# Two batches through attention and MLP layers: side work of one batch placed between the attention slots of the other

## The chip, the cores and the metric

One NeuronCore of a Trainium2 chip. The metric is the device time of one execution in microseconds (us). Several executions of a kernel are timed and their median is given; one further execution is profiled, and all rows in this document come from profiled executions.

## The reference, cut to what matters

B = 2 batches, S = 512 tokens, D = 128 features. `x` passes through four conditioned layers; the change touches only what follows layer 0.

```python
def L1(x, c):                       # attention over all tokens, then a 4-chunk MLP
    h = ln(x) * (1 + scale_msa) + shift_msa
    q, k, v = split(h @ w_qkv)      # 16 heads of 8 features
    x = x + gate_msa * (softmax(q @ k.T * 8 ** -0.5) @ v @ w_proj + b_proj)
    h2 = ln(x) * (1 + scale_mlp) + shift_mlp
    return x + gate_mlp * (gelu(h2 @ w_fc1 + b_fc1) @ w_fc2 + b_fc2)

def L2(x, t, mask):                 # two 2-chunk MLPs, the first one masked
    norm = where(m, ln(x) * (1 + scale) + shift, 0)
    x = x + gate * where(m, gelu(norm @ ssm_w1 ..) @ ssm_w2 + gelu(norm @ bwd_w1 ..) @ bwd_w2, 0)
    return x + gate_mlp * (gelu_tanh(ln'(x) @ ff_w1 + ff_b1) @ ff_w2 + ff_b2)

def L3(x, c):                       # as L1, but the attention is causal
    ...
```

## The kernel before, in words

Every engine runs its own instruction stream; they wait for one another on semaphores. Layer 0 (quantised products, a scan, a gated MLP) takes the first 170 us and is the same before and after.

Then comes a sequence of six blocks, `SEQ` (line 213): number 0, attention of layer 1, called here the open attention (a = 0); numbers 1, 2 and 3, MLPs of 4, 2 and 2 chunks of 128 hidden features; number 4, the causal attention of layer 3 (a = 1); number 5, a 4-chunk MLP. Each block is done for both batches before the next one begins. Chunks are columns of the hidden layer: a first-layer product (L1376) makes one chunk for all 512 tokens, an activation (L1186) applies Gelu or its tanh form and writes `hid`, and the second-layer products (L1529) make the result, four token tiles by as many chunks. Each batch's MLP is preceded by a norm: statistics on VectorE (L516, L519, L521), the inverse root on GpSimd (L344), the normalised `xn` on VectorE (L526), four transposes on TensorE (L1247), and the modulated `hT` on ScalarE (L1125).

An attention has eight units, four heads of one batch each; units 0 to 3 are batch 0, units 4 to 7 batch 1. A unit has eight slots, each with two score products in bf16 (L1497, keys by queries) and two exponentials on ScalarE (L1173). Every second slot completes a key tile, whose product with the values, P·V (L1475, fp32), is accumulated in one bank over four key tiles. In the causal attention key tile kt concerns only queries from 128 kt on, so its score products, exponentials and P·V are 512, 384, 256 and 128 wide, and GpSimd zeroes the triangle first (L440).

The exponentials need each row's maximum beforehand. It is taken from a second set of score products, queries by keys (L1451; in the causal attention with a mask product, L1454), by a VectorE reduction (L932): eight steps per unit, six in the causal attention. GpSimd splits the maxima into bf16 parts (L430 to L432), TensorE transposes them (`parts`, L1421), VectorE copies them, and SyncE writes them by DMA into rows of `QZ` (L329), so that the score product subtracts the maximum itself. q and k stand in `QZ` and `KZ` as three bf16 pieces each: ScalarE makes the high part (L1136) and the middle (L1140), VectorE the rests (L808, L812), and SyncE copies the pieces into place with twelve DMAs per batch (L321), issued one after the other.

PSUM has eight banks. Three (2, 3, 4) hold scores for the exponentials, one (5) the accumulated output, and two pairs (0 and 1, 6 and 7) are a ring (`RING`, line 237). Every other result in an attention is a ring item and takes the next pair in turn; a new item waits for what was read out of the item two before it (`consumed`, line 1395).

The order of the ring items is written out by `schedule` (line 240): the maxima run 12 steps ahead of the slots (9 in the causal attention), the split maxima are transposed one maximum after a unit is complete (`LAG`, line 228), the output of a unit is transposed and divided in slot 5 of the unit after next, and a few items of batch 0 come early (`EARLY`, line 230): its output transposed in slot 52, its projection in 54, its next norm transposed in 59. P·V is issued in two halves of the queries (`probs_out`, line 1458), one per slot, from three or four slots behind (`LATE`, line 229). ScalarE copies the output of unit u-1 before the exponentials of slot 3 of unit u (`unit_out`, line 1141). Before ScalarE changes its function a small activation loads the function table ahead of need (`table`, line 1043).

GpSimd also adds the gated bias to `x` (`add_bias`, line 393). For MLP 2 it does so tile by tile, a product with the mask (L398) and an add (L399), sixteen instructions, each waited for.

```python
SEQ = ((0, "att", 1), (1, "mlp", 1), (2, "mlp", 2), (3, "mlp", 3), (4, "att", 3), (5, "mlp", 5))
advance(min(ahead + ((s + 1) * n + 7) // 8 - (0 if s >= 39 else 0), first + (s + 1) * n // 5))
for s in range(64):
    # two score products, then the ring items of the slot, then half a P.V
```

## Time and profile before

| what | value |
|---|---|
| median of 3 timed executions | 490.38 us (489.73 to 490.95) |
| profiled execution, own time | 488.39 us |
| profiled execution, span of its instructions | 486.6 us |
| mean granted TensorE clock | 0.825 of full |
| layer 0 and the first q, k, v | 0 to about 175 us |
| exponentials of the open attention | 195.4 to 285 us |
| MLPs 1 to 3, second q, k, v, first causal maxima | 285 to 360 us |
| exponentials of the causal attention | 360.4 to 461.3 us |
| output, projection, last MLP, store | 461.3 to 486.6 us |

Times in rows are microseconds from the first instruction of the span. Own time less span, 1.8 us, lies outside the instructions. A group row counts one line of the kernel on one engine; `L1475 x8` are eight instructions, since an fp32 product is two. The granted clock is TensorE's: 1.00 is 2.4 GHz and 0.50 is 1.2 GHz. In a chain, each piece is what the next one waited for.

### The profile page before, as it was taken

The numbers are of one execution on the slowest core, as the hardware profiler recorded it, in microseconds if no ns is written. First come the engines' busy times: TensorE is split into PE (matmuls) and PEld (weight loads), VectorE is DVE, ScalarE is ACT, GpSimd is POOL, SyncE is SP. The second block draws the span as 40 slices with busy tenths as digits, with TensorE's granted clock in tenths as the row PEclk, the third lists the DMA queues.
The fourth block names the chain that finished last, engine by engine and source line by source line (L and its number), as shares of the span: only waits on it lengthen the run. The fifth ranks groups of instructions, "written<-read, shape, count | busy, mean of one in ns | idle before, by whom it ended". The sixth has DMA issues, their size and how long they took to land.

```text
span 486.6 us, 6451 instructions
## 1 busy us (share of the span) xinstructions
PE 317.5 (65%) x2274; PEld 148.4 (31%) x2274; DVE 303.9 (62%) x683; ACT 251.0 (52%) x550; POOL 121.9 (25%) x184
## 2 busy tenths in 40 slices
PE   0015844621245563988988888758678977788786
PEld 0004613511103420222222345535222232333354
DVE  0778787759588659888888314346675354554230
ACT  3267645562466212788887773333435354456542
POOL 0112139640363510000000202563012222222410
PEclk9999965555557756799999999989757598889799
DMA  7940350000000233000000000000710000000001
GB/s 243 417 186 0 130 223 0 1 0 0 1 0 1 68 99 92 2 3 3 1 2 2 2 2 1 0 1 20 198 43 2 1 2 3 2 1 2 1 1 43
DMA packets 11652, 21.90 MB, mean 45 GB/s; under 512 B 2010, under 2 KB 10462, under 8 KB 10846
## 3 DMA queue, kind: packets, MB, share of 16 engines
q1 hardware_dynamic: 11620, 21.49, 12.8%
q8 instruction: 18, 0.29, 0.2%
q14 instruction: 14, 0.11, 0.1%
HBM read 14.54 MB, written 0.52 MB: 31 GB/s over the span
## 4 chain that ended last, share of the span: by engine, by line
PE 41%; DVE 24%; ACT 18%; POOL 6%; issue 6%; DMA 2%; SPq 2%; DVEq 0%; ACTq 0%; POOLq 0%
PE pe L1475 10%; ACT big L1173 8%; PE pe L1497 6%; DVE nm L932 5%; PE pe L1376 4%; PE pe L1529 4%; PE pe L1451 4%; PE pe L1454 3%; PE pe L1247 2%; POOL rstd L344 2%; ACT scr L1058 2%; PE pe L1341 2%; PE pe L1426 1%; DVE st L516 1%; DVE xn L526 1%
## 5 line engine op out<-in xcount | busy, mean ns | idle before, releaser
L1173 ACT ACTIVATE big<-pe 128x512 f32<-128x512 f32 (+3 forms) x256 | 116.7, 521 | 81.6 <-PE pe L1497 80.4
L932 DVE TENSOR_REDUCE nm<-pe 128x2 f32<-128x1024 f32 (+2 forms) x112 | 124.2, 1145 | 50.1 <-PE pe L1454 38.1
L1475 PE MATMUL pe<-big,scr 128*32 128x256 f32 (+4 forms) x896 | 74.1, 408 | 3.8 <-ACT scr L1146 2.6
L1451 PE MATMUL pe<-big 62*128 62x512 bf16 (+3 forms) x256 | 53.1, 395 | 15.9 <-DVE nm L932 13.0
L1497 PE MATMUL pe<-big 64*128 64x512 bf16 (+3 forms) x256 | 54.9, 371 | 8.4 <-ACT big L1173 7.0
L344 POOL TENSOR_TENSOR rstd<-var,half 128x4 f32<-128x4 f32 x26 | 28.5, 1097 | 110.5 <-DVE var L521 85.9
L440 POOL TENSOR_SCALAR_AFFINE_SELECT big<-big 128x512 f32<-128x512 f32 x32 | 20.3, 635 | 73.4 <-ACT big L1173 73.4
L1497 PEld LDWEIGHTS pe<-big 64*128 64x128 bf16 x256 | 15.7, 94 | 64.7 <-ACT big L1173 33.5
L430 POOL CAST nm<-nm 128x16 bf16<-128x16 f32 x16 | 3.1, 196 | 102.0 <-DVE nm L932 102.0
L526 DVE TENSOR_SCALAR xn<-x_tok,mv,rstd 128x128 f32<-128x128 f32 x64 | 18.6, 353 | 15.7 <-POOL rstd L344 15.7
L1475 PEld LDWEIGHTS pe<-big,scr 128*32 128x32 f32 x896 | 18.9, 111 | 29.2 <-issue 12.3
L1125 ACT ACTIVATE hT<-pe,modc 128x512 f32<-128x512 f32 x12 | 9.4, 779 | 34.7 <-PE pe L1247 34.7
L1247 PE MATMUL pe<-ident,xn 128*128 128x128 f32 x48 | 9.4, 330 | 26.7 <-ACT xn L1058 13.6
L1376 PE MATMUL pe<-hT,w 128*128 128x512 f32 x48 | 24.5, 636 | 3.5 <-ACT hT L1125 3.5
L1247 PE MATMUL pe<-ident,scr 128*128 128x128 f32 x48 | 12.8, 431 | 19.2 <-ACT scr L1058 18.2
L1186 ACT ACTIVATE scr<-pe,col 128x512 f32<-128x512 f32 x24 | 16.3, 688 | 14.6 <-PE pe L1376 14.6
L1451 PEld LDWEIGHTS pe<-big 62*128 62x128 bf16 x256 | 13.4, 98 | 30.0 <-DVE nm L932 20.6
L1454 PE MATMUL pe<-cmask 128*128 128x128 bf16 x128 | 21.5, 260 | 0.0
L955 DVE RECIPROCAL rec<-pe 128x16 f32<-128x16 f32 x16 | 4.0, 252 | 22.6 <-PE pe L1426 22.6
L1050 ACT ACTIVATE junk<-scr 128x128 f32<-128x128 f32 x24 | 7.1, 297 | 20.6 <-DVE scr L649 20.5
L1058 ACT ACTIVATE scr<-scr,magic,q 128x128 f32<-128x128 f32 x32 | 12.7, 480 | 9.5 <-DVE q L670 9.5
L969 DVE TENSOR_TENSOR x_tok<-x_tok,pe 128x512 f32<-128x512 f32 x6 | 4.1, 688 | 21.1 <-PE pe L1529 21.0
(188 smaller groups left out, 560.3 us busy)
## 6 DMA issues: line engine op xcount, KB each, us to landing
big<-tern SPq DMA_DIRECT2D x48, 128.0 KB, 2.4
big<-in_fill SPq DMA_DIRECT2D x1, 4096.0 KB, 13.6
big<-in_wa SPq DMA_DIRECT2D x1, 2304.0 KB, 12.5
w<-in_w SPq DMA_DIRECT2D x2, 1152.0 KB, 19.2
big<-in_wa SPq DMA_DIRECT2D x1, 1344.0 KB, 6.2
big<-in_w SPq DMA_DIRECT2D x1, 1024.0 KB, 14.4
w<-in_w SPq DMA_DIRECT2D x1, 896.0 KB, 19.8
rowg<-in_rowg SPq DMA_DIRECT2D x1, 832.0 KB, 18.4
```

Of the source, the lines that this page charges most:

```text
L344: nc.gpsimd.tensor_tensor(dst, src, half[0:src.shape[0], 0:n], ALU.pow).then_inc(sem(done), 1)
L440: nc.gpsimd.affine_select(block_, block_, [[0, HG], [1, 128]], ALU.is_ge, zero, base=0, channel_multiplier=-1).then_inc(sem("triangle"), 1)
L526: last = v.tensor_scalar(xn[:, t], x_tok[:, t], mv[:, t, 0:1], rstd[:, t:t + 1], ALU.subtract, ALU.mult)
L932: v.tensor_reduce(dst, src[:, :, 0:w * len(pairs)].rearrange("p r (h w) -> p r h w", w=w), AX.X, ALU.max, negate=True).then_inc(sem(f"a{a} ...
L1058: last = s_.activation(dst[:, t], src[:, t], ACT.Identity, bias=magic[:, 0:1], scale=q4[:, 3, m, t:t + 1])
L1173: s_.activation(P[:, kt % PRING, 2 * p + j, q0:S], bank[SINGLES[i % 3]][:, q0:S], ACT.Exp, scale=SCALE).then_inc(sem(f"a{a}_p"), 1)
L1247: last = t_.transpose(bank[bk][:, i * D:(i + 1) * D], src[:, t], ident[:])
L1376: t_.matmul(bank[2 + i % 4], m["w"][:, m["at"] + c * D:m["at"] + (c + 1) * D], hT[:, b], start=True, stop=True).then_inc(sem("n_h"), 1)
L1451: last = t_.matmul(dsts[par][:, k * wd:(k + 1) * wd], QZ[rows, b, 2 * g + i, qt * 128:(qt + 1) * 128], KZ[rows, b, 2 * g + i, 0:wd], start ...
L1454: last = t_.matmul(dsts[par][:, (k + 1) * wd - 128:(k + 1) * wd], cmask[:, 0], cmask[:, 1], start=False, stop=True)
L1475: last = t_.matmul(bank[PV_BANK][32 * h:32 * h + 32, lo:hi], V[b][:, kt, HG * g + h, :], P[:, k % PRING, h, lo:hi], start=(kt == 0), stop= ...
L1497: last = t_.matmul(bank[SINGLES[(2 * s + j) % 3]][:, q0:S], KZ[rows, b, 2 * g + p, kt * 128:(kt + 1) * 128], QZ[rows, b, 2 * g + p, q0:S], ...
```

## The change

The whole of `SEQ` is replaced by one list of events, `ORDER`, made by `work_order()`, that all five engines walk. Between the slots of an attention stand events of the MLPs (`SIDE`), for a batch whose attention is already done:

- in the open attention, batch 0 (units 0 to 3) is done by slot 37. Its projection comes in slots 38 to 40, its MLP 1 from slot 43, MLP 2 from 52, MLP 3 from 60 to 63, while batch 1's attention goes on;
- between the two attentions (`GAP`) stand the norm and q, k, v of batch 0 and the projection of batch 1. Ahead of the first causal slot, among ten causal maxima of batch 0, batch 1's norm and first-layer products of MLP 1 (`BEFORE`);
- in the causal attention slots 0 to 26 also carry batch 1's MLP 1 result, MLPs 2 and 3, its norm, q, k, v and its pieces (`stack`). The causal maxima of batch 1 may not start before slot 27 (`GATE`), then two per slot;
- batch 0's projection and MLP 5 stand in causal slots 38 to 49; batch 1's follow alone at the end (`TAIL`).

Every product of this side work is a ring item now. A four-chunk MLP makes its first-layer products two chunks at a time, in two consecutive slots (`in`), and its result in two halves in two slots (`res`, `res2`). Within a slot ScalarE does the exponentials first and then the Gelus, with no explicit table load except the first one; the compiler places the others. Counted along `ORDER`, ScalarE changes between exponential and Gelu, or its tanh form, 19 times; before there are four such loads in this part.

Further: P·V is issued whole every second slot, five slots behind at most (`LATE` 3 and 5); the output's copy (`evict`) follows directly on the unit's last P·V; the maxima run 13 and 10 ahead; the split maxima are transposed two maxima after the unit is complete, or two slots later if no maxima come. The masked bias of MLP 2 is computed once, eight products on GpSimd before `ORDER`, and added by one instruction. The semaphores of batch 0 and batch 1 are separate.

```diff
-        SEQ = ((0, "att", 1), (1, "mlp", 1), (2, "mlp", 2), (3, "mlp", 3), (4, "att", 3), (5, "mlp", 5))
-        LAG = 1
-        LATE = (3, 4)
-        EARLY = {52: "o_turn", 54: "proj", 59: "n_turn"}
+        AHEAD, LAG, LATE, GATE = (13, 10), 2, (3, 5), 27
+        def mlp(n, b, at):
+            ins = [("in", n, b, c) for c in range(0, MLPS[n]["n"], 2)]
+            k = at + 2 + len(ins)
+            return placed({at: [("xn", n, b)], at + 1: [("turn", n, b)], at + 2: [("bias", n, b)]},
+                          {at + 3 + i: [x] for i, x in enumerate(ins)},
+                          {k + 1: [("res", n, b)], k + 2: [("res2", n, b), ("add", n, b)]})
+        def projected(n, b, at):
+            return {at: [("oturn", n, b)], at + 1: [("res", n, b), ("res2", n, b)], at + 2: [("add", n, b)]}
+        BEFORE = ({1: [("q1",)], 2: [("k1",)], 3: [("v1",), ("q1_less",)], 4: [("q1_low",)], 5: [("k1_low",)]},
+                  {2: [("root", 1, 1)], 5: [("xn", 1, 1), ("turn", 1, 1)], 6: [("bias", 1, 1)],
+                   7: [("in", 1, 1, 0)], 8: [("in", 1, 1, 2)]})
+        SIDE = (placed(projected(0, 0, 38), {41: [("root", 1, 0)]}, mlp(1, 0, 43), {50: [("root", 2, 0)]},
+                       mlp(2, 0, 52), {58: [("root", 3, 0)]}, {60: [("xn", 3, 0)], 61: [("turn", 3, 0)],
+                       62: [("bias", 3, 0), ("in", 3, 0, 0)], 63: [("res", 3, 0), ("res2", 3, 0), ("add", 3, 0)]}),
+                placed({0: [("res", 1, 1)], 1: [("res2", 1, 1), ("add", 1, 1)], 2: [("root", 2, 1)]},
+                       mlp(2, 1, 4), {11: [("root", 3, 1)]}, mlp(3, 1, 12), {19: [("root", 4, 1)]},
+                       {21: [("xn", 4, 1)], 22: [("turn", 4, 1)], 23: [("bias", 4, 1), ("qk", 1, 1)],
+                        24: [("stack", 1, 1, 0), ("less", 1, 1), ("v", 1, 1)], 25: [("mid", 1, 1), ("vals", 1, 1)],
+                        26: [("low", 1, 1), ("stack", 1, 1, 1), ("stack", 1, 1, 2)]},
+                       projected(4, 0, 38), {41: [("root", 5, 0)]}, mlp(5, 0, 43)))
+        GAP = [("root", 4, 0), ("evict", 0, 7), ("out", 0, 7), ("xn", 4, 0), ("turn", 4, 0), ("bias", 4, 0), ("oturn", 0, 1),
+               ("qk", 1, 0), ("res", 0, 1), ("res2", 0, 1), ("stack", 1, 0, 0), ("less", 1, 0), ("mid", 1, 0), ("v", 1, 0),
+               ("vals", 1, 0), ("low", 1, 0), ("stack", 1, 0, 1), ("stack", 1, 0, 2), ("add", 0, 1)]
...
+        def work_order():
+            ev = []
+            for a in range(2):
+                n, at, due, age = len(STEPS[a]), 0, [], 0
+                for s in range(-1, 64):
+                    if s >= 0:
+                        ev.append(("exp", a, s))
+                        if a == 1 and s % 2:
+                            ev.append(("triangle", s // 2))
+                    until = AHEAD[a] + max(0, ((s + 1) * n + 7) // 8)
+                    if a == 1 and s < GATE:
+                        until = min(until, 4 * n)
...
+                        ev.append(("max", a, at // n, at % n))
...
+                        if due and at % n == LAG:
+                            ev.append(("parts", a, due.pop()))
+                        if at % n == 0:
+                            ev.append(("pieces", a, at // n - 1))
...
+                        if s >= 0 and done == 2:
+                            break
...
+                    if s >= 8 and s % 8 == 5:
+                        ev.append(("out", a, s // 8 - 1))
+                    ev += SIDE[a].get(s, ())
+                    k = (s - LATE[a]) // 2
+                    if s >= LATE[a] and (s - LATE[a]) % 2 == 0:
+                        ev.append(("pv", a, k))
+                        if k % TB == TB - 1:
+                            ev.append(("evict", a, k // TB))
...
-                if n == 2:
-                    for t in tiles(b):
-                        link(nc.gpsimd.tensor_scalar(junk[:, 0:D], gate_bias(n, b), maskf[:, t:t + 1], None, ALU.mult))
-                        last = nc.gpsimd.tensor_tensor(x_tok[:, t], x_tok[:, t], junk[:, 0:D], ALU.add)
-                        link(last)
+            for t in range(B * TB):
+                link(nc.gpsimd.tensor_scalar(mask_bias[:, t], gate_bias(2, t // TB), maskf[:, t:t + 1], None, ALU.mult))
...
+                elif kind == "in":
+                    n, b, c0 = e
+                    dsts = consumed(("in", n, b, c0))
+                    m = MLPS[n]
+                    pe.wait_ge(sem(f"hT{b}"), n + 1)
+                    for c in range(c0, c0 + 2):
+                        last = t_.matmul(dsts[c - c0], m["w"][:, m["at"] + c * D:m["at"] + (c + 1) * D], hT[:, b],
+                                         start=True, stop=True)
+                    last.then_inc(sem("ring"), 1)
```

## Rows read from the trace of the kernel before

**Rows 1.** The page, busy time by engine:

```profile
PE 317.5 (65%) x2274; PEld 148.4 (31%) x2274; DVE 303.9 (62%) x683; ACT 251.0 (52%) x550; POOL 121.9 (25%) x184
```

**Rows 2.** Chain, open attention: start us, us, engine line:

```profile
232.17 0.49 ACT scr L1146
...
232.79 1.07 PE pe L1475 x8
...
266.25 1.06 PE pe L1475 x8
...
278.66 1.07 PE pe L1475 x8
```

**Rows 3.** Groups by form, 195 to 286: count, busy us, mean ns, idle before:

```profile
L932 DVE TENSOR_REDUCE nm<-pe 128x2 f32<-128x1024 f32 x53 | 61.9, 1220 | 7.4 <-PE pe L1451 6.3 <-POOL nm L432 0.9
```

**Rows 4.** Windows: length, then PE, PEld, DVE, ACT, POOL busy, clock, DMA:

```profile
239.00:250.00 11.00, 9.77 (x95) 2.78 (x93) 9.75 (x12) 8.92 (x17) 0.61 (x3) 1.00 0.01 2
...
310.00:324.00 14.00, 6.92 (x45) 5.19 (x45) 6.57 (x28) 5.07 (x7) 10.85 (x18) 0.99 0.01 1
...
349.00:366.00 17.00, 13.90 (x75) 4.20 (x73) 12.30 (x13) 4.47 (x10) 2.19 (x7) 0.50 0.26 72
366.00:400.00 34.00, 28.90 (x275) 10.29 (x275) 16.83 (x23) 14.99 (x41) 7.71 (x18) 0.77 0.01 2
```

**Rows 5.** Timeline of TensorE between the attentions, the two products of MLP 1:

```profile
298.33 3.70 PE L1376 MATMUL pe<-hT,w 128*128 128x512 f32 x8 [0.87 <-ACT hT L1125]
302.81 3.84 PE L1529 MATMUL pe<-wg,scr 128*128 128x128 f32 x32 [0.78 <-ACT scr L1186]
```

**Rows 6.** Chain, batch 0's second q, k, v (eleven transfers from 338.14 on):

```profile
335.54 0.79 ACT hT L1125
...
338.14 0.59 SPq L321
...
345.21 2.38 DMA big<-tern
```

**Rows 7.** Timeline of ScalarE, from the last open to the first causal exponentials:

```profile
282.75 2.14 ACT L1173 ACTIVATE big<-pe 128x512 f32<-128x512 f32 x4
...
286.69 1.28 ACT L1045 ACT_TABLE_LOAD   x1
287.98 0.20 ACT L1045 ACTIVATE warm<-ones 128x1 f32<-128x1 f32 x1
...
302.07 0.69 ACT L1186 ACTIVATE scr<-pe,col 128x512 f32<-128x512 f32 x1 [0.17 <-PE pe L1376]
...
360.38 2.30 ACT L1173 ACTIVATE big<-pe 128x512 f32<-128x512 f32 x4 [11.78 <-PE pe L1497]
```

**Rows 8.** Chain, causal attention:

```profile
366.73 1.71 PE pe L1475 x8
...
379.20 1.79 PE pe L1475 x8
...
394.19 0.97 PE pe L1475 x8
...
404.34 0.63 POOL big L440
...
405.83 0.27 PE pe L1421
406.09 1.79 PE pe L1475 x8
```

**Rows 9.** Timeline of VectorE, one add and norm of MLP 1:

```profile
297.06 0.69 DVE L969 TENSOR_TENSOR x_tok<-x_tok,pe 128x512 f32<-128x512 f32 x1 [1.87 <-PE pe L1529]
...
300.41 1.11 DVE L526 TENSOR_SCALAR xn<-x_tok,mv,rstd 128x128 f32<-128x128 f32 x4 [1.13 <-POOL rstd L344]
```

**Rows 10.** Chain, the end:

```profile
461.34 0.64 POOL big L440
...
483.13 0.69 DVE x_tok L969
```

831 lines of the change are left out of this document (398 added, 433 removed).

## The prediction

> **What bounds the kernel now.** I read the page first, for which engine is busiest: TensorE, at 65% [rows 1]; no engine is full, so the limit changes by stage. The windows by stage come next, then the chain of waits inside each stage, then single engines in time order.
>
> In the open attention (195 to 286 us) three units, 232.79 to 266.25, take 33.46 us, 11.15 each [rows 2]. Per slot VectorE has one maximum of 1.22 us [rows 3] and ScalarE two exponentials; in 239 to 250 VectorE is 9.75 of 11 us busy, ScalarE 8.92, TensorE 9.77 [rows 4]: three engines near 89% that wait for one another. ScalarE's copy of the output (0.49 us on the chain, just ahead of TensorE's next P·V) is one of the waits [rows 2]. Where such a unit also holds the projection and norm of batch 0 (266.25 to 278.66) it takes 12.41 us although it has only one maximum: side work adds to a unit here, it is not free.
>
> From 286 to 360.4 us no exponential runs: the MLPs of both batches, the second q, k, v, and the splits. The reader should see three things: TensorE's two products of a four-chunk MLP take 3.70 and 3.84 us [rows 5]; GpSimd's masked bias is 10.85 us busy in 14 [rows 4]; and after the modulated activations (335.54) SyncE issues one transfer each 0.64 us, eleven from 338.14, and the last lands at 347.59 [rows 6]. Then come nine maxima before the first exponential at 360.38 [rows 7], at a granted clock of 0.50, the 1.2 GHz level, after that idle stretch; it is 0.77 in 366 to 400 [rows 4].
>
> In the causal attention a unit takes 406.09 - 394.19 = 11.9 us here, and its 64 slots 100.9 us, 12.6 per unit. TensorE works almost without a break from 394.19 to 402.84, bar a wait of about 1.3 for a maximum; then the last exponentials, GpSimd's triangle (404.34), its split of the maxima and their transpose (405.83) pass one after the other before P·V can go on: 3.25 us in which TensorE does little [rows 8].
>
> **The change part by part**, against the profiled execution (span 486.6, own time 488.39; the median of the runs, 490.38, is 2 above). A margin of 0.3%, 1.5 us, is about what a measurement of this kernel can tell from no change.
>
> *Open attention, slots 0 to 37.* The first maxima are turned after ten maxima instead of nine: +1.2, one maximum. P·V is issued whole every second slot, and the output is copied two slots before its bank is needed: the unit can come down towards the 9.9 that VectorE is busy in it, but TensorE's 1.07 us lump may starve ScalarE. Bounds -3 to +3; I take -0.25 per unit, -1.2. Sum 0.
>
> *Open attention, slots 38 to 63, batch 0's side work.* Projection: +1.3 (0.99 of TensorE for the product, a transpose and a copy). Each MLP: +0.6 for its turned slot, hT being 0.79 [rows 6]. The four-chunk MLP, slots 46 to 49: ScalarE's functions alternate, so each `in` slot is exponentials, load 1.28, two Gelus 1.38, load 1.28 [rows 7]. The second `in` waits for the first one's bank; the first half of the result waits for the last Gelu. Followed on TensorE and ScalarE: first `in` ready at 2.3, its Gelus done at 4.0, second `in` at 5.7, exponentials 47 at 6.4, Gelus at 9.0, half result 10.9, other half 13.4, P·V 14.5, copy 15.1. Four slots take 14.9 in place of 5.6: +9.3. A two-chunk MLP the same way takes 7.9 in place of 4.2: +3.7. The third MLP's exponentials 63 come +3.6 later. Sum with three turned slots: 1.3+1.8+9.3+3.7+3.6 = +19.7. TensorE's own work in these items is 18, so this side work is hardly hidden.
>
> *The hole.* Slot 62 starts at about 282.2 before (its exponentials are on ScalarE from 282.75 [rows 7]) and 16.1 later, at 298.3, after. In it: product ready at 2.0, Gelus at 4.0, result at 6.1, then add, statistics, root and xn as in [rows 9], where 297.06 to 301.52 spans one such norm, 4.5; turn 0.6 and activation 0.8: hT at 310.2. q and k are now one ring item (1.8, and 0.6 for the first copy), so the first transfer goes out at 312.6; twelve by 0.64 and 2.4 to land: 322.7, against 347.6. **-24.9.** The two batches' other MLPs and the masked bias (now computed once, ahead of the loop, under the ring's first maxima, at nothing; if GpSimd were late there, eight by 0.6 = 5) are what leaves.
>
> *Before the first causal exponential*: 12.8 before. After, ten maxima share VectorE with batch 1's norm, TensorE with its turn and four products (3.7 warm, 7.4 at 1.2 GHz), and the turned maxima wait behind the first Gelus. Bounds 16 to 24, I take 19.5: exponentials start at 342.2 instead of 360.4. Net so far **-18**.
>
> *Causal slots themselves.* The split of the maxima gets two further maxima of lead, the copy two slots, the triangle one half slot. TensorE's 8.65 less 0.45 for the undivided P·V, plus one maximum, the transpose and the divided output gives 8.8 per unit; with ScalarE's wide slots I take 9.75, or 78 for 64 slots, against 100.9: **-23**. Bounds: 8.8 (-30) and no change (0). I lean to the low end because the three waits on the chain are just those given lead. Being TensorE-bound, the stage now pays for the low clock: +4.
>
> *Side work in the causal slots.* Result of batch 1's first MLP, 3.84 in slots 0 and 1: +3.6. Its second and third MLP: +4.2 each. q, k, v: +2.3. Its twelve transfers: 13.1 us from slot 23 to landing, against some 7 until slot 27, where TensorE stops at the first maximum of batch 1, and everything behind it in its queue (exponentials' scores, P·V) stops too: +5.5. Two maxima a slot in 27 to 31: +1.5. Projection and last MLP of batch 0: +9.9. Sum **+31.2**.
>
> *Tail.* Last triangle at 461.34 to end of the last add 483.13+0.69: 22.5 [rows 10]. After, batch 0's MLP is gone, but batch 1's chain (output, projection 0.99, norm 4.5, turn, hT 0.79, products 3.5, Gelus 1.4, result 3.84, add 0.7) is serial and sums to 21.1: **-1.4**.
>
> Sum: -18 -23 +4 +31.2 -1.4 = -7.2, so 488.4 - 7.2 = 481.2 against the profiled execution, and **483** against the median, which is 2 above it.
>
> **Where rule and row differ.** Fifteen table loads are added (19 in this part after, 4 before). The trace shows a load of 1.28 us with the next activation 0.01 us after its end [rows 7], and the sum uses that. The Trainium skill, page "ScalarE: Activation LUTs", section "What ACT_TABLE_LOAD costs", puts a drain of 1.38 us beside the same 1.28. By it fifteen loads would cost up to 20.7 more; the rows here show no such drain.
>
> **Rivals.**
> A, *the causal slots do not shorten* (slower). Place: the ring of two bank pairs between TensorE, VectorE and GpSimd in the causal loop. If a new item there, a norm or an add waiting on VectorE, blocks the ring as the split does now, the unit stays between 11.5 and 12.6: +14 to +23, so 497 to 506. It decides from 10.7 us a unit on, where the -7.2 is used up. For it: the unit from 366.73 to 379.20 took 12.5 us, that from 394.19 to 406.09 took 11.9 [rows 8], though the clock was 0.77 in the first stretch [rows 4], so waits, not work, set it, and the change adds waits. Against: those on the chain are addressed. 0.27.
> B, *the side work fills TensorE's gaps*. Then the causal part tends to TensorE's work, 70 + 25 + 4 = 99 in place of 113, and slots 38 to 63 grow by 12.5, not 19.7: 21 less, 462. For it: ScalarE and VectorE are 44 to 50% busy in 366 to 400 [rows 4]. Against: the unit of 12.41 us. 0.20.
> C, *each change of function stalls ScalarE longer than its load*, which a busy pipeline could show where these rows, with ScalarE mostly idle, do not: fifteen more gaps of a load's own length, 1.28, are 19: 502. It is the rule above. 0.04.
> D, *the sides cancel* within 1.5 us of 490: the transfers of batch 1 land 7 us later still. 0.05.
> Forecast 0.44, own range 475 to 491.
>
> **How the numbers follow.** B reaches down to 462 and A up to 506. Leaving out the lower edge of B and the upper half of A and C gives 464 to 498. Faster: 0.39 of the forecast and B: 0.60. Within 0.3%: D and a little of the forecast: 0.08. Slower: 0.32.
>
> **What would show it.** First causal exponential near 342; the last open one near 304.7; causal unit near 9.75 without side work; 19 table loads of 1.28 from slot 46 on and nothing behind them; TensorE idle about 5 us before the first maximum of batch 1; last triangle to end of the last add 21. The prediction is wrong if the causal units stay above 11, or if slots 46 to 49 take 11 instead of 15.

## The result, and the profile after

The changed kernel takes **524.01 us** (522.94 to 524.5) where the kernel before takes 490.06 (489.27 to 490.95) beside it: ratio 1.0689, 95% interval 1.0664 to 1.0715. The prediction, 483.0 with a range of 464 to 498, was wrong in sign and in size. Executions more than 1.5% above the fastest of their kernel are left out of the ratios: two of the four without table loads (521.8 and 522.0), one of four with the split maxima one maximum later (505.2) and one of ten with that in the causal attention alone (490.4); what sets them apart was not found. The profiled execution of after has an own time of 524.5 and a span of 522.8, 36.2 more than before.

Busy time by engine in the kernel after, from its page; it answers to [rows 1]:

```profile
PE 332.1 (64%) x1889; PEld 150.0 (29%) x1890; DVE 303.5 (58%) x683; ACT 266.3 (51%) x561; POOL 121.1 (23%) x178
```

TensorE has 385 instructions fewer (the undivided P·V) and is busy 14.6 us longer, ScalarE, with the added table loads, is busy 15.3 us longer; the other engines have the same work. Where the added 36.2 us are is read from four marks in each trace: the last exponential of the open attention, the first and the last of the causal attention, the end of the last add.

| stage | before | forecast change | measured after | measured change |
|---|---|---|---|---|
| to the end of the open exponentials | 284.9 | +19.8 | 315.4 | +30.5 |
| from there to the first causal exponential | 75.5 | -38.0 | 43.5 | -32.0 |
| causal exponentials | 100.9 | +12.2 | 133.5 | +32.6 |
| from there to the end of the last add | 22.5 | -1.4 | 27.6 | +5.1 |

The four misses are 10.7, 6.0, 20.4 and 6.5 us. Their sum is 43.6; the span was 43.4 over the -7.2 of the forecast. The hole did shrink, nearly as far as forecast. What left it was paid for again, and more, in the attentions.

One number made all causal units comparable: ScalarE copies the output once per unit. The copies of units 1 to 3 and then 4 and 5 of the kernel before start at 391.06, 402.91, 416.06 and 429.27, 442.04, so 11.9 to 13.2 apart. ScalarE in time order, kernel after, the copies of open units 1 and 2 (start, length, line, form, and in brackets the idle time before and its releaser):

```profile
221.07 0.59 ACT L1203 COPY scr<-pe 128x512 f32<-128x512 f32 x1 [0.26 <-PE pe L1460]
228.06 2.06 ACT L1190 ACTIVATE big<-pe 128x512 f32<-128x512 f32 x4 [1.77 <-PE pe L1443]
230.73 2.06 ACT L1190 ACTIVATE big<-pe 128x512 f32<-128x512 f32 x4 [0.60 <-PE pe L1443]
233.05 0.59 ACT L1203 COPY scr<-pe 128x512 f32<-128x512 f32 x1 [0.26 <-PE pe L1460]
...
270.61 1.08 ACT L1190 ACTIVATE big<-pe 128x512 f32<-128x512 f32 x2 [2.69 <-PE pe L1443]
271.71 1.28 ACT L1216 ACT_TABLE_LOAD   x1
273.01 1.27 ACT L1216 ACTIVATE scr<-pe,col 128x512 f32<-128x512 f32 x2
274.29 1.28 ACT L1190 ACT_TABLE_LOAD   x1
275.59 1.09 ACT L1190 ACTIVATE big<-pe 128x512 f32<-128x512 f32 x2
276.69 1.28 ACT L1216 ACT_TABLE_LOAD   x1
277.99 1.27 ACT L1216 ACTIVATE scr<-pe,col 128x512 f32<-128x512 f32 x2
279.27 1.28 ACT L1190 ACT_TABLE_LOAD   x1
280.56 2.30 ACT L1190 ACTIVATE big<-pe 128x512 f32<-128x512 f32 x4
285.00 0.59 ACT L1203 COPY scr<-pe 128x512 f32<-128x512 f32 x1 [2.14 <-PE pe L1460]
...
423.68 0.59 ACT L1203 COPY scr<-pe 128x512 f32<-128x512 f32 x1 [7.19 <-PE pe L1460]
```

Three things. An open unit without side work takes 11.98 (221.07 to 233.05), not 10.9: ScalarE now idles 1.77 and 0.60 us for scores, which it gets behind an undivided P·V. Slots 46 to 49, 270.61 to the first exponential of slot 50 at 285.49, take 14.9 us with four table loads in them, as worked out; the loads last 1.28 each and the next activation starts 0.02 later. And the third causal unit ends with ScalarE idle for 7.19 us.

One part of the open attention's length is not the order of the work. Slots 38 to 45 of the kernel after, and the same slots of an experiment below whose lists are the same up to there (the last MLP of batch 0 at the end), columns as in [rows 4]:

```profile
252.00:270.60 18.60, 13.99 (x87) 4.61 (x85) 13.13 (x25) 10.01 (x19) 2.92 (x5) 0.91 0.01 1
```

```profile
252.80:269.80 17.00, 12.38 (x87) 4.25 (x85) 13.04 (x25) 10.01 (x19) 2.91 (x5) 1.00 0.01 1
```

The same instructions take 1.6 us less at a granted clock of 1.00 than at 0.91. Three kernels with these lists (the last MLP at the end, the norm ahead, no wait for pieces) take 117.3 to 117.4 us from the first to the last open exponential, the profiled execution of after 119.6. So some 2.3 of its 36.2 us are this execution's clock, and each comparison of a trace with it holds them.

The windows of the kernel after, columns as in [rows 4]: slots 46 to 49, the unit with batch 1's transfers, the unit with two maxima per slot, slots 43 to 50, the serial end, and the causal part in three stretches:

```profile
270.60:285.50 14.90, 12.22 (x75) 5.94 (x73) 6.39 (x9) 12.50 (x18) 0.00 (x0) 1.00 0.00 0
...
402.00:424.00 22.00, 14.55 (x92) 5.83 (x88) 6.88 (x17) 9.71 (x25) 5.38 (x7) 0.77 0.27 73
424.00:442.00 18.00, 15.95 (x113) 5.22 (x112) 12.14 (x16) 6.40 (x18) 3.54 (x10) 0.72 0.01 1
456.00:479.00 23.00, 19.36 (x123) 10.02 (x119) 8.37 (x13) 14.68 (x26) 4.83 (x9) 0.85 0.04 10
492.40:510.00 17.60, 9.71 (x47) 5.72 (x40) 3.77 (x16) 3.23 (x5) 2.92 (x3) 0.50 0.00 1
...
358.90:400.00 41.10, 35.24 (x237) 16.86 (x239) 21.46 (x49) 23.71 (x47) 11.24 (x19) 0.83 0.01 1
400.00:440.00 40.00, 30.68 (x203) 10.85 (x195) 19.75 (x38) 15.63 (x40) 8.63 (x17) 0.74 0.15 41
440.00:492.40 52.40, 41.92 (x309) 18.71 (x311) 19.34 (x39) 31.84 (x74) 13.08 (x26) 0.90 0.02 6
```

Where side work stands, TensorE is busy more than four fifths of the time (19.36 of 23.00; 12.22 of 14.90, with ScalarE at 12.50), so a product of the side work has no idle TensorE to go to. In the transfers' unit everybody waits (TensorE 14.55 of 22.00). The serial end runs at 0.50, the 1.2 GHz level. The last three rows are kept for the comparison with an experiment: TensorE is busy 107.8 of 133.5 us in the causal part.

TensorE in time order, kernel after, the first maximum of each batch:

```profile
335.61 0.29 PE L1421 MATMUL pe<-big 62*128 62x128 bf16 x2 [7.02 <-DMA big<-tern]
...
420.55 0.29 PE L1421 MATMUL pe<-big 62*128 62x128 bf16 x2 [4.82 <-DMA big<-tern]
```

The second one is the wait that the prediction placed here, 4.8 against "about 5".

The chain of waits of the kernel after, slots 43 to 50 and the end:

```profile
462.86 1.79 PE pe L1532 x4
464.67 1.27 ACT scr L1216 x2
465.95 1.28 ACT L1190
...
469.00 1.27 ACT scr L1216 x2
470.41 2.49 PE pe L1484 x16
...
508.00 6.05 PE pe L1532 x8
514.07 0.69 ACT scr L1216
```

Product, Gelu, table load, exponentials, Gelu, result: the side chain and the attention's chain run through each other, one after the other. At the end the four-chunk first layer takes 6.05 us, against 3.70 in [rows 5].

### The profile page after: what moved, and what is told of

Its sections match the earlier page's. It is cut to its first block and busy times, and to the rows that moved or that the text cites. A ratio compares the mean times of both kernels' runs of the same rounds, so it can differ in the third digit from the quotient of the medians.

```text
span 522.8 us, 5677 instructions
## 1 busy us (share of the span) xinstructions
PE 332.1 (64%) x1889; PEld 150.0 (29%) x1890; DVE 303.5 (58%) x683; ACT 266.3 (51%) x561; POOL 121.1 (23%) x178
## 3 DMA queue, kind: packets, MB, share of 16 engines
q1 hardware_dynamic: 11620, 21.49, 11.9%
## 5 line engine op out<-in xcount | busy, mean ns | idle before, releaser
L948 DVE TENSOR_REDUCE nm<-pe 128x2 f32<-128x1024 f32 (+2 forms) x112 | 125.8, 1146 | 84.7 <-PE pe L1424 60.7
L1190 ACT ACTIVATE big<-pe 128x512 f32<-128x512 f32 (+3 forms) x256 | 114.5, 524 | 73.2 <-PE pe L1443 72.8
L1421 PE MATMUL pe<-big 62*128 62x512 bf16 (+3 forms) x256 | 54.2, 393 | 28.3 <-DVE nm L948 12.3
L1443 PE MATMUL pe<-big 64*128 64x512 bf16 (+3 forms) x256 | 61.6, 366 | 14.0 <-ACT big L1190 13.4
L1460 PE MATMUL pe<-big,scr 128*32 128x512 f32 (+3 forms) x512 | 65.9, 595 | 0.0
L475 POOL TENSOR_SCALAR_AFFINE_SELECT big<-big 128x512 f32<-128x512 f32 x32 | 20.4, 638 | 100.7 <-ACT big L1190 100.7
L1532 PE MATMUL pe<-hT,w 128*128 128x512 f32 x48 | 28.0, 717 | 3.2 <-DVE nm L948 1.1
L1421 PEld LDWEIGHTS pe<-big 62*128 62x128 bf16 x256 | 13.1, 97 | 46.4 <-DVE nm L948 20.1
L1282 PE MATMUL pe<-ident,scr 128*128 128x128 f32 x48 | 12.8, 431 | 20.5 <-ACT scr L1096 19.5
L975 DVE TENSOR_TENSOR x_tok<-x_tok,pe 128x512 f32<-128x512 f32 x10 | 6.8, 683 | 27.2 <-PE pe L1484 27.2
L1468 PE MATMUL pe<-ident,xn 128*128 128x128 f32 x56 | 11.6, 349 | 16.4 <-DVE xn L567 12.7
L1216 ACT ACTIVATE scr<-pe,col 128x512 f32<-128x512 f32 x24 | 15.2, 684 | 12.2 <-PE pe L1532 12.1
L1203 ACT COPY scr<-pe 128x512 f32<-128x512 f32 x16 | 9.5, 592 | 18.2 <-PE pe L1460 18.2
L1282 PE MATMUL pe<-ident,xn 128*128 128x128 f32 x16 | 4.4, 431 | 21.0 <-ACT xn L1096 13.6
## 6 DMA issues: line engine op xcount, KB each, us to landing
w<-in_w SPq DMA_DIRECT2D x2, 1152.0 KB, 19.2
w<-in_w SPq DMA_DIRECT2D x1, 896.0 KB, 19.8
rowg<-in_rowg SPq DMA_DIRECT2D x1, 832.0 KB, 18.1
```

The source lines that it names most:

```text
L475: nc.gpsimd.affine_select(block_, block_, [[0, HG], [1, 128]], ALU.is_ge, zero, base=0, channel_multiplier=-1).then_inc(sem("triangle"), 1)
L948: v.tensor_reduce(dst, src[:, :, 0:w * len(pairs)].rearrange("p r (h w) -> p r h w", w=w), AX.X, ALU.max, negate=True).then_inc(sem("max"), 1)
L1190: s_.activation(P[:, kt % PRING, 2 * p + j, q0:S], bank[SINGLES[i % 3]][:, q0:S], ACT.Exp, scale=SCALE).then_inc(sem("p"), 1)
L1216: s_.activation(hid[:, b, c], bank[PLACE["in", n, b, c0] + c - c0], m["func"], bias=col[:, m["bias"] + c:m["bias"] + c + 1]).then_inc(sem( ...
L1421: last = t_.matmul(dsts[par][:, k * wd:(k + 1) * wd], QZ[rows, b, 2 * g + h, qt * 128:(qt + 1) * 128], KZ[rows, b, 2 * g + h, 0:wd], start ...
L1443: t_.matmul(bank[SINGLES[i % 3]][:, q0:S], KZ[rows, b, 2 * g + p, kt * 128:(kt + 1) * 128], QZ[rows, b, 2 * g + p, q0:S], start=True, stop ...
```

## The experiments

The theories were: **T1**, side work costs its full serial time, since the engines that it needs are the ones that bound the attention; **T2**, the causal ring still blocks and the unit does not shorten (rival A); **T3**, table loads are the price; **T4**, the undivided P·V; **T5**, the wait for batch 1's transfers. A kernel whose name begins with "before" is an edit of the kernel before; the others are edits of the kernel after. The copies' distance is called the unit.

### P·V in halves again

```diff
-                    if s >= LATE[a] and (s - LATE[a]) % 2 == 0:
-                        ev.append(("pv", a, k))
...
+                    k, part = (s - LATE[a]) // 2, (s - LATE[a]) % 2
+                    if s >= LATE[a]:
+                        ev.append(("pv", a, k, part))
...
```

> The changed kernel with P·V issued in two halves again, one per slot, as before the change; everything else of the change stays. Theory 1, the lump: a whole P·V of 1.07 us leaves ScalarE without scores (its idle time is 0.6 and 1.8 us in turn in the open units, which take 11.98 us where they took 11.15). Then the open units go back to about 11.2 and the time falls by 8 to 12 us, to 512 to 516. Theory 2, the ring: a maximum or another ring item at the head of TensorE's queue sets the slots and the lump only fills that wait: within 2 us of 524.

518.66 us (518.17 to 519.48), ratio 1.061 [1.0582, 1.0638]. The open units fall from 11.98 to 11.08 (209.43, 220.51, 231.60), below the 11.15 of before. So T4 is right in the free units. By the medians it is worth 5.3 of the 34, less than the 8 to 12 expected. The traces give less still: from the first to the last open exponential 115.2 us, against 117.3 to 117.4 in the three kernels named above, so 2.1. The unit with MLP 1 takes 26.4 us with halves (at a granted clock of 0.87) and 23.6 without (at 1.00), and that gives most of the free units' gain back.

### The kernel before with P·V undivided

```diff
-                        lo, hi = (q0, S if kt == 0 else mid) if part == 0 else (mid, S)
-                        if kt == 0 and part == 1:
+                        lo, hi = q0, S
+                        if part == 1:
...
```

> The kernel before with P·V issued whole in the slot of its first half, nothing else changed. Theory 1: the open units rise from 11.15 towards 12, the causal ones by as much or less, so 6 to 13 us slower, 496 to 503. Theory 2: within 2 us of 490.

497.16 us, ratio 1.0176 [1.0147, 1.0205]. The same lump costs 8.5 us there, and all of it in the open attention: its units take 12.43 instead of 11.15, and it is 8.5 us longer from its first to its last exponential, while the causal exponentials take 99.8 us, against 100.9 before.

### No change of function

```diff
-                s_.activation(hid[:, b, c], ..., m["func"],
+                s_.activation(hid[:, b, c], ..., ACT.Identity,
```

This leaves the non-linearity of all MLPs of this part out, and with it the table loads.

> The changed kernel with Gelu and its tanh form replaced by the identity with the same bias, which needs no other function table: the MLPs' non-linearity is left out. Sixteen of the 19 table loads stand among exponentials, 1.28 us each, 20.5 us together. If ScalarE is what the side work waits for, as the prediction's working of slots 46 to 49 has it, most of that comes back: 506 to 512. If TensorE and the ring set the side slots, under half comes back: 515 to 522.

509.6 and 510.1 us; the ratio, 1.0428 [1.0388, 1.0468], puts the loads at some 13 of the 34. Slots 43 to 50 take 19.1 instead of 23.0. The open part ends 6.9 us earlier; against the three kernels at the full clock it is 5.0 shorter, so part of the 13 may be clock. T3 is a part of it: 13 us for the added loads, which last 15 by 1.28 = 19.2. They are partly hidden, and nothing comes on top of them.

### Both products of a four-chunk MLP in one slot

```diff
-            k = at + 2 + len(ins)
+            k = at + 3
...
-                          {at + 3 + i: [x] for i, x in enumerate(ins)},
+                          {at + 3: ins},
```

> The changed kernel with both first-layer products of a four-chunk MLP in one slot, twice among the attention slots, so four table loads of 1.28 us fewer, and the result one slot earlier. If ScalarE's loads set these slots: 4 to 6 us faster, 518 to 520. If the ring sets them (the second product then waits for the maximum between), within 2 us of 524.

520.43 us, ratio 1.061 [1.0574, 1.0646]: 3.6 less than after, for four table loads (5.1 us) fewer. So the separate slots that the change gives the two products cost a little instead of bringing anything.

### The split maxima one maximum later, kernel before

```diff
-        LAG = 1
+        LAG = 2
```

> The kernel before with the split maxima transposed two maxima after a unit is complete instead of one, in both attentions. The prediction's term of -23 us for the causal slots rests on this lead. If TensorE's wait for the split (1.5 us per causal unit) is a real limit, 6 to 12 us faster: 478 to 484. If another wait takes its place at once (the ring holds only two items, so a later transpose blocks the same bank), within 2 us of 490.

499.96 us, ratio 1.0171 [1.0123, 1.0219]. That is outside both ranges expected. Six causal units take 76.8 instead of 79.1, 0.4 each; at the same granted clock of 1.00 a unit takes 11.7 here and 11.8 before, so even the 0.4 is mostly clock. The open units grow to between 12 and 13.6, at a clock of 0.87: there the transpose of the maxima now falls into the slot that transposes the output, and both are ring items. The lead of the split was the first of three reasons that the prediction gave for shorter causal units; alone it brings next to nothing.

### Batch 0's last MLP at the end

```diff
-                       projected(4, 0, 38), {41: [("root", 5, 0)]}, mlp(5, 0, 43)))
+                       projected(4, 0, 38), {41: [("root", 5, 0)], 43: [("xn", 5, 0)], 44: [("turn", 5, 0)],
+                       45: [("bias", 5, 0)]}))
...
-        TAIL = [("evict", 1, 7), ("out", 1, 7), ("oturn", 4, 1), ("res", 4, 1), ("res2", 4, 1), ("add", 4, 1), ...
+        TAIL = [("evict", 1, 7), ("in", 5, 0, 0), ("out", 1, 7), ("in", 5, 0, 2), ("oturn", 4, 1), ...
```

> The changed kernel with batch 0's last MLP taken out of causal slots 46 to 49 (its norm and turn stay in 41 to 45) and put between the steps of batch 1's output and projection at the end, where the kernel before had it. The eight causal slots 43 to 50 took 23.0 us with it and 12.8 before. Theory 1, side work placed among slots adds its full time while the end is a chain of waits that would hide it: the slots fall to about 14, the end grows by 2 to 5, so 4 to 8 us faster, 516 to 520. Theory 2, the causal slots are slow by themselves in the changed kernel: they stay above 18 and the time rises by 2 to 5.

508.86 us, ratio 1.0393 [1.037, 1.0416], 15 less than after. Three us of it lie ahead of slot 0, where the two kernels are alike (first causal exponential at 355.9 instead of 358.9), most of them the clock in the open attention. The rest is this: slots 43 to 50 take 12.6 instead of 23.0, and the end, with twice the work in it, takes 26.9 instead of 27.9. ScalarE in time order and the windows of this kernel (slots 43 to 50; the end):

```profile
454.17 0.58 ACT L1204 COPY scr<-pe 128x512 f32<-128x512 f32 x1 [0.81 <-PE pe L1461]
466.75 0.58 ACT L1204 COPY scr<-pe 128x512 f32<-128x512 f32 x1 [0.19 <-PE pe L1461]
```

```profile
484.00:508.00 24.00, 14.67 (x92) 10.90 (x90) 4.50 (x16) 5.05 (x8) 2.28 (x2) 1.00 0.08 23
454.20:466.80 12.60, 10.50 (x84) 3.87 (x80) 7.50 (x12) 7.08 (x19) 4.87 (x10) 0.86 0.00 1
```

So a four-chunk MLP costs 10.4 us among causal slots (TensorE is 19.36 us busy there against 10.50, so 8.9 of it are its own products, the rest waits). Beside the other batch's serial end it costs nothing here, but the clock is part of that: 1.00 in this end and 3.69 us for the product (494.67) that took 6.05. Against the shortest end without it, 25.3 us at 0.81 in the kernel with both products in one slot, it costs 1.6, the rest being covered by the other chain's waits. T1 stands.

### Batch 1's norm and turn ahead of the first causal maximum

```diff
-                  {2: [("root", 1, 1)], 5: [("xn", 1, 1), ("turn", 1, 1)], 6: [("bias", 1, 1)],
-                   7: [("in", 1, 1, 0)], 8: [("in", 1, 1, 2)]})
+                  {2: [("in", 1, 1, 0)], 4: [("in", 1, 1, 2)]})
```

with root, xn, turn and bias of (1, 1) appended to `GAP`.

> The changed kernel with batch 1's first norm and turn moved ahead of the first causal maximum, and its first-layer products moved from the 8th and 9th to after the 2nd and 4th maximum. TensorE waits 7.0 us there for batch 0's transfers, and afterwards VectorE, TensorE and ScalarE pass the norm, the turn and the products to each other between maxima; the first causal exponential comes 23.3 us after the transfers land, 12.8 before. If that stretch is a chain of waits, 4 to 8 us faster: 516 to 520. If the first products now only delay the maxima, within 2 us of 524.

525.02 us (518.48 to 525.23), ratio 1.0683 [1.0611, 1.0754]: no gain by the median, though one of the four executions took 518.48 and the others 524.9 to 525.2. The forecast of 516 to 520 missed. In the profiled execution the stretch between the attentions did get shorter, 40.7 us against 42.5 in the kernel above and in the one below, which are alike up to there. But the seventh causal unit then took 11.4 us at a granted clock of 0.56, where it takes 8.3 at 1.00 in the kernel after. So this run doesn't refute that an earlier norm shortens the start-up; it shows that the clock can take more than that back.

### Without the wait for batch 1's pieces

```diff
-                if i == 0 and g == 0:
+                if i == 0 and g == 0 and not (a and b):
...
+                b = 0 if a else b
...
```

The causal scores of batch 1 are computed from batch 0's pieces, in the maxima and for the exponentials; batch 1's own are copied but unused.

> The changed kernel with the causal scores of batch 1 taken from batch 0's pieces, so that nothing waits for batch 1's twelve transfers; the pieces are still made and moved. The prediction had this wait at 5.5 us; the trace shows TensorE idle for 4.8 us there, ScalarE 7.2, and a lower clock after it. If the wait and the clock behind it are the cause of the 18.1 and 21.4 us of those two units, 6 to 10 us faster: 514 to 518. If the two maxima a slot set them, within 3 us of 524.

516.71 us, ratio 1.0553 [1.0525, 1.0582]: 7.3 less than after. The unit is 15.3 (400.61 to 415.91) instead of 21.4, so 6.1 are the wait's; in the traces the rest lies ahead of slot 0. T5 is right, near its forecast price of 5.5. The unit behind it, with two maxima per slot, stays at 17.9 (18.1 in the kernel after): its length does not come from the wait. TensorE is busy in it 15.95 of 18.00 us at a clock of 0.72 in the kernel after.

### Halves and the last MLP at the end together

Both edits above.

> The changed kernel with P·V in halves and batch 0's last MLP at the end, the two parts undone that gave 5 and 15 us alone. If they are independent: 524 - 5 - 15 = 504. If both only warm TensorE's clock at the end, less than the sum: 507 to 509.

510.47 us, ratio 1.0421 [1.0382, 1.046]. Alone they brought 5.3 and 15.2; together 13.5, more than the 504 of two independent parts, and over the 507 to 509 of the other case. The traces of this kernel and of the one with the last MLP at the end say where the halves' gain goes: open exponentials 115.2 us against 117.4, causal ones 123.1 in both, and 29.6 instead of 28.1 behind them (at a granted clock of 0.95 instead of 1.00). Of the 5.3, 2.1 are then the halves' in the open attention, and the end gives 1.5 back.

### All MLPs between the attentions, the batches in turn

```diff
+        GAP = [("evict", 0, 7), ("in", 1, 0, 0), ("out", 0, 7), ("in", 1, 0, 2), ("oturn", 0, 1), ("res", 0, 1), ...
+               ("res", 1, 0), ("res2", 1, 0), ("root", 1, 1), ("xn", 1, 1), ("turn", 1, 1), ("bias", 1, 1), ("add", 1, 0),
+               ("root", 2, 0), ("in", 1, 1, 0), ("in", 1, 1, 2), ("xn", 2, 0), ...
...
-        AHEAD, LAG, LATE, GATE = (13, 10), 2, (3, 5), 27
+        AHEAD, LAG, LATE, GATE = (13, 10), 2, (3, 5), 0
```

Beside the two edits above. MLPs 1 to 3 and both q, k, v stand in `GAP`, one step of batch 0, then one of batch 1; the slots keep only the projections and the next norm of batch 0.

> As the kernel with halves and batch 0's last MLP at the end, and all MLPs of layers 1 and 2 and both batches' second q, k, v stand between the two attentions, the two batches in turn; the lists, the lead of the maxima (13 and 10) and the once-computed masked bias of the change stay. Theory 1, side work among slots costs its full time or more: it returns to the time of the kernel before or a little below, 484 to 492, so 12 to 20 us faster than with the MLPs among the slots. Theory 2, interleaving them pays and the loss lies in the new order of ring items: 503 or slower.

492.9 us (488.99 to 494.8), ratio 1.0061 [1.0035, 1.0087]. Seventeen of the 20 us left over come back. ScalarE in time order of this kernel, copies of causal units 2 to 4:

```profile
412.14 0.59 ACT L1195 COPY scr<-pe 128x512 f32<-128x512 f32 x1 [0.33 <-PE pe L1457]
421.92 0.59 ACT L1195 COPY scr<-pe 128x512 f32<-128x512 f32 x1 [0.33 <-PE pe L1457]
438.01 0.57 ACT L1195 COPY scr<-pe 128x512 f32<-128x512 f32 x1
```

and its windows, the gap, two free causal units and the whole causal part:

```profile
290.20:375.90 85.70, 57.97 (x308) 36.23 (x308) 40.12 (x128) 24.91 (x36) 16.64 (x17) 0.86 0.14 38
402.40:421.90 19.50, 17.88 (x220) 7.25 (x218) 13.66 (x19) 13.20 (x34) 6.22 (x14) 1.00 0.01 2
376.00:464.00 88.00, 77.10 (x776) 29.25 (x780) 47.15 (x73) 52.95 (x137) 26.05 (x54) 0.83 0.01 2
```

A causal unit without side work takes **9.77**, where 9.75 was forecast, with TensorE 17.88 of 19.50 us busy. So T2 is refuted as far as the free unit goes: it does shorten. The whole causal part takes 88 us, with TensorE 77.1 busy and 10.9 idle; in the kernel after it takes 133.5, with 107.8 busy and 25.7 idle. So of the 45 us that side work costs there, 31 are TensorE's own time for it and 15 are new waits, 6.1 of them the transfers'. (The later maxima of batch 1, `GATE`, went with the side work, so the 45 hold their price too; it was not taken apart.) The next thing to see is the unit of 438.01 - 421.92 = 16.1, which holds the projection and norm of batch 0: +6.3 for work that the open side's forecast puts at 1.9. TensorE in time order in it:

```profile
430.54 0.39 PE L1413 MATMUL pe<-big 62*128 62x512 bf16 x2 [1.13 <-DVE x_tok L967]
...
436.67 0.63 PE L1466 MATMUL pe<-ident,xn 128*128 128x128 f32 x4 [1.25 <-DVE xn L559]
```

A maximum waits for the add of the projection, and the transposes, a ring item, for the norm; TensorE is busy 11.63 of 16.10 us, at a granted clock of 1.00. This is the mechanism that rival A named, a norm or an add that waits on VectorE and holds the ring. It does not lengthen all units, but it does lengthen those that carry such an item. The gap is 85.7, against 75.5 before, although its order was made so that the batches cover each other.

### Batch 0's MLPs among the open slots, batch 1's alone in the gap

```diff
+                placed(projected(4, 0, 38), {41: [("root", 5, 0)], 43: [("xn", 5, 0)], 44: [("turn", 5, 0)],
+                       45: [("bias", 5, 0)]}))
+        GAP = [..., ("add", 0, 1), ("root", 1, 1), ("xn", 1, 1), ("turn", 1, 1), ("bias", 1, 1), ("in", 1, 1, 0), ("in", 1, 1, 2),
+               ("res", 1, 1), ("res2", 1, 1), ("add", 1, 1), ("root", 2, 1), ...]
```

Batch 0's MLPs stay among the open slots; batch 1's follow in the gap, alone, then its q, k, v.

> As the kernel with halves and batch 0's last MLP at the end (510), but batch 1's MLPs of layers 1 and 2 and its second q, k, v come all before the causal attention, one step after the other; batch 0's stay among the open slots. With all of them between the attentions, in turn with batch 0's, the time was 492.9. Batch 1's chain alone has 3.84 + 3.70, twice 1.9 + 2.05, four norms of 4.5 and q, k, v behind it, some 45 us, partly beside the first transfers; the causal side work it takes away is worth about 31. If a batch alone is the loss, slower than 510: 514 to 524. If the causal slots are where side work costs most, faster: 498 to 508.

512.2 us, ratio 1.0466 [1.0427, 1.0506], between the two ranges expected. The causal part is 83.2 (399.95 to 483.1), but the gap is 88 us long, as long as with both batches in it. One window of it:

```profile
325.00:365.00 40.00, 18.82 (x72) 11.18 (x72) 11.84 (x48) 6.90 (x10) 6.84 (x6) 0.75 0.12 33
```

TensorE, the busiest, works less than half of the time. Batch 0's MLPs cost the open slots 22 us (their last exponential ends at 312.1, against 290.2 in the kernel above) and taking them out of the gap buys nothing: a lone batch's chain is as long as the two in turn. This is the second half of T1. The clock has a share in it that was not taken apart: 0.74 in this gap, 0.86 in the gap with both batches.

### The kernel before with the masked bias computed once

```diff
-                    for t in tiles(b):
-                        link(nc.gpsimd.tensor_scalar(junk[:, 0:D], gate_bias(n, b), maskf[:, t:t + 1], None, ALU.mult))
-                        last = nc.gpsimd.tensor_tensor(x_tok[:, t], x_tok[:, t], junk[:, 0:D], ALU.add)
+                    nc.gpsimd.tensor_tensor(x_tok[:, bt(b)], x_tok[:, bt(b)], mask_bias[:, bt(b)], ALU.add)
```

> The kernel before with the masked bias computed once ahead of the attention and added in one instruction per batch, nothing else changed. GpSimd's sixteen small instructions (309.97 to 320.0) held the root of the next norm and the adds of MLP 2. That is on the chain for 3 to 6 us: 483 to 487. If the products of the other batch covered it, within 1 us of 489.

485.55 us, ratio 0.9908 [0.9877, 0.9939]: 4.5 faster than the kernel before. It is one of two parts of the change found to gain by themselves; the other is the later causal P·V below.

### The same, with the transpose of the causal maxima one maximum later

```diff
-                    if at > n and at % n == LAG:
+                    if at > n and at % n == (1 if n == 8 else 2):
```

> The kernel before with the masked bias computed once, and the split maxima transposed two maxima after a unit in the causal attention only. With lag 2 in both, six causal units took 76.8 us where they took 79.1; the open ones lost because the transposed maxima fell into the same slot as the output. If that is right, 2 to 3 us below the 485.5 of the masked bias alone: 482 to 484. If not, 485 to 487.

486.26 us (482.42 to 490.44), ratio 0.9933 [0.9895, 0.997]. No gain over the bias alone; the lead of the split is not what shortens the causal unit, even where the open attention is spared the collision.

### The same, with causal P·V and the output's copy later

```diff
-        LATE = (3, 4)
+        LATE = (3, 5)
...
-                if kt == 1 and p == 1 and u >= 1:
+                if kt == 1 + causal and p == 1 and u >= 1:
```

on top of the bias alone.

> The kernel before with the masked bias computed once and the causal P·V five half slots behind instead of four, with the output's copy one key tile later. Causal units without side work took 9.8 us in the changed lists with halves, 12.6 before. If the distance between exponentials, triangle and P·V is what shortens them: 10 to 20 us faster than 485.5, so 466 to 476. If the lead of the maxima does, within 3 us of 485.5.

**471.74 us** (471.05 to 472.09), ratio 0.964 [0.9618, 0.9662]: faster than both kernels. The copies of its causal units, ScalarE in time order:

```profile
397.33 0.58 ACT L1148 COPY scr<-pe 128x512 f32<-128x512 f32 x1 [1.41 <-PE pe L1477]
407.53 0.59 ACT L1148 COPY scr<-pe 128x512 f32<-128x512 f32 x1 [1.42 <-PE pe L1477]
```

and its chain of waits, end of one unit and start of the next; it answers to [rows 8]:

```profile
404.69 0.88 ACT big L1175 x2
...
405.63 0.63 POOL big L442
406.26 0.15 POOL nm L432
...
406.77 0.21 POOL nm L434
...
407.11 0.22 PE pe L1423
...
408.89 0.99 PE pe L1477 x8
```

The wait for the split maxima is still there (404.69 to 407.11), but the unit is 10.2 instead of 12.6: one slot more between the triangle and the P·V that needs it, and the later copy, take other waits away. Two windows of the kernel before, at different granted clocks, and one of this kernel, each one unit, columns as in [rows 4]:

```profile
391.10:402.90 11.80, 9.24 (x110) 3.93 (x109) 6.80 (x10) 6.46 (x17) 3.10 (x7) 1.00 0.01 2
416.10:429.30 13.20, 10.77 (x110) 4.11 (x109) 6.85 (x10) 6.50 (x18) 3.10 (x7) 0.87 0.01 2
```

```profile
397.30:407.50 10.20, 9.08 (x113) 3.72 (x109) 6.87 (x10) 6.55 (x17) 3.10 (x7) 1.00 0.01 3
```

At the same clock of 1.00 the unit falls from 11.8 to 10.2, and TensorE's idle time in it from 2.6 to 1.1 us. The rest of the 2.4 us is the clock, which was below 1.00 in most units before and is 1.00 in the free units here. Why it stays up was not tested.

### Lag of two, and ten maxima ahead, on top

```diff
-                    if at > n and at % n == LAG:
+                    if at > n and at % n == (1 if n == 8 else 2):
```

> The same, and the split maxima transposed two maxima after a unit in the causal attention. If both waits had to go together (each takes the other's place), 10 to 20 us faster than 485.5 here and not in the kernel with one of them alone: 466 to 476. If neither matters, 483 to 488.

476.25 us, ratio 0.9735 [0.9713, 0.9756]: 4.5 slower than without it.

```diff
-            ahead = n + n // 2
+            ahead = n + n // 2 + (n == 6)
```

> The same, and the causal maxima ten steps ahead instead of nine: all three settings of the change's causal attention in the old structure, MLPs between the attentions. If the three together make the 9.8 us unit, 466 to 476, below both kernels. If only the ten steps matter, this one alone of the three is that fast.

476.11 us, ratio 0.973 [0.9708, 0.9752]: the further maximum changes nothing. With the edit before, the free units are 10.7 and 10.5. The 9.77 of the kernel with all MLPs between has a third ingredient, which was not isolated.

## Why the prediction was wrong

The steps, in its own order, with the miss of each against the profiled execution (the measured time less the forecast's):

- **Open slots 0 to 37, "sum 0"**: +3.1 (slot 38 begins at 252.0 instead of 248.9). The copy's lead brought nothing, and the undivided P·V cost 0.9 per unit (two experiments). The risk was named ("may starve ScalarE"), and the wrong side taken. With halves slot 38 begins at 248.3, so this term would have held.
- **Slots 38 to 63, +19.7**: slots 46 to 49 took the 14.9 of the forecast, but they took 4.5 before, not the 5.6 of its sum (260.06 to 264.55), so their term is 1.1 short. Slots 38 to 45 took 18.6 where 13.0 was forecast; 1.6 of that is the granted clock of 0.91, since the same slots take 17.0 at 1.00. Projection, norm and turn were priced by TensorE's time, +1.3 and +0.6. Each is a chain of ScalarE, VectorE and TensorE items in a ring of two places, and the slots behind it wait: ScalarE's two idles before `hT` and the exponentials behind it are 2.07 and 2.69 us, and 2.07 and 1.15 at the full clock. In the causal slots the price of projection and norm is 6.3.
- **The hole, first transfers**: the pieces landed 20.1 us after the last open exponential, 18.0 forecast: 2.1 late. The start-up behind it took 23.4 instead of 19.5, inside its bounds; with batch 1's norm earlier the whole stretch was 1.7 shorter than in its equals.
- **Causal slots themselves, -23**: right in size for a free unit (9.77 against 9.75). The prediction credited three leads together, for the split maxima, the copy and the triangle. The runs show that the later P·V, which is the triangle's lead, and the copy carry it: 12.6 to 10.2 with them alone, 0.4 with the split's lead alone. And it left out that the length before held a low clock: 1.6 of the 2.4 us remain at the full clock. That the size came out so near is in part luck.
- **Side work in the causal slots, +31.2, with +4 for the clock**: this is the failed step. The kernel with only projections there needs 88.2 for the 64 slots, the kernel after 133.5: 45.3 for the MLPs, q, k, v, transfers and late maxima, where about 34 stood in the sum with the clock. And the 88.2 is itself nearly 9 more than the forecast's 78 with a projection of 1.3. What failed is that each item was priced by its own durations: its waits in the ring, and what the slots behind it lose, were put at nothing, except for the transfers, which came out near (6.1 against 5.5). By units, taken against those of the kernel with all MLPs between: slots 0 to about 27 cost +28.6 where the terms give 19.8; the unit with two maxima per slot +8.3 where 1.5 was taken, at a granted clock of 0.72; the last MLP +10.4 in its unit.
- **Tail, -1.4**: +5.1. The forecast's 21.1 is a sum of durations at 2.4 GHz; the stretch ran at 0.50 (6.05 for the product at 3.5 forecast, 2.76 for 24 P·V instructions). At 0.81, in the kernel with both products in one slot, the same stretch takes 23.8, so of the miss of 6.5 the clock accounts for 3.8 or more, and up to 2.7 are open. That the end is shorter when batch 0's MLP is gone holds only at a better clock: with the MLP in it, at 1.00, it is 26.9; without it 27.9 at 0.50 and 25.3 at 0.81.
- **Table loads**: nineteen by 1.28, nothing behind them, as the row said, also in a busy pipeline. Taking them out returned some 13 us; the 20.7 that the Trainium skill's page "ScalarE: Activation LUTs", section "What ACT_TABLE_LOAD costs", would have added on top is not seen. Rival C is false.

Of the rivals, A comes nearest. Its condition, a free unit that stays between 11.5 and 12.6, did not come; its mechanism, a norm or an add that waits on VectorE and holds the ring, did, in the units that carry such items, and there costs 6.3 us for one projection and norm. Its bound of 506 was too low. The case that happened, side work costlier than its TensorE time on both sides at once, had no rival of its own: the prediction had doubts only about the unit without side work, and a rival (B) for side work that would be cheaper. The evidence against that stood in [rows 2]: 12.41 for a unit with a projection, a norm and one maximum against 11.15. The prediction's +1.3 is no more than that difference. But that unit lacks seven of its eight maxima; a unit without maxima and without side work takes 9.85 (273.43 to 283.28 in the kernel with all MLPs between), so the price shown there was at least 2.6.

The account of the 34 us on the chip:

| kernel | us | what it says |
|---|---|---|
| after | 524.0 | |
| P·V in halves | 518.7 | lump: 5.3 by the medians, 2.1 by the traces of the open attention |
| no wait for batch 1's pieces | 516.7 | 7.3, of which 6.1 in the unit that waits |
| no table loads | about 510 | about 13 |
| last MLP of batch 0 at the end | 508.9 | 15.2 |
| all MLPs between, two batches in turn, halves | 492.9 | 31.1: side work among the slots is the loss |
| before with the bias once and P·V later | 471.7 | what the new schedule has that gains |

The rows overlap, so they aren't summed. Open: what the clock by itself is worth in each row, what the later maxima of batch 1 cost apart from the side work, why one execution of the kernel with the norm ahead took 518.5 and three took 525, and what takes the causal unit from 10.2 to 9.77.

## What to carry to other kernels

Putting independent work into the slots of a pipeline is free only where an engine that it needs is idle in that stretch; where TensorE alone needs 17.9 of 19.5 us it costs all its TensorE time and its waits on top, 10.4 us here for an MLP whose products took 8.9, and 45 us for all of the side work, of which 31 were TensorE's. An item that waits, a norm or an add, costs more than its work when other items queue behind it: 6.3 us for a projection and a norm. Two batches in turn cover each other's waits, so taking one of them away leaves the other's chain at full length: 88 us with one batch in the gap, 85.7 with two. Look first for more distance between a producer and its consumer: one slot more ahead of P·V, and the later copy with it, brought 14 us for two edited lines. And read the granted clock beside each stretch before comparing two traces: the same slots took 18.6 us at 0.91 and 17.0 at 1.00.
